# A decoder's first cross-attention: keys and values projected one stage earlier, during the state-space loop

## What is computed

```python
x = x + mamba(layernorm(x))          # per step: h = exp(delta*A)*h + delta*B*u ; y = sum over 8 states of C*h
# first cross-attention, 16 heads of 16
Q = layernorm(x) @ wq.T + bq
K = ctx @ wk.T + bk                  # ctx: 375 rows for each of 32 batch elements
V = ctx @ wv.T + bv
att = softmax(where(mask == 0, -1e-9, Q K^T / sqrt(16)))
x = x + (att @ V) @ wo.T + bo
x = x + switch_ffn(layernorm(x)); x = x + agent_attention(layernorm(x))
x = x + second_cross_attention(layernorm(x), ctx)   # other weights, same context
x = x + latent_moe(layernorm(x))
```

## Time and profile before

| | |
|---|---|
| median of 3 runs | 2842.92 us (2836.62 to 2844.70) |
| the profiled execution, its own time | 2844.52 us |
| its span, first to last instruction | 2842.7 us |
| TensorE busy | 2446.9 us (86%) |
| VectorE busy | 1947.9 us (69%) |
| ScalarE busy | 1565.1 us (55%) |
| bytes moved by DMA | 168.10 MB |

### The profile page before, as it was taken

One profiled execution on the slowest core, in us unless ns is written; L12 is line 12 of the kernel. 1 busy time (PEld: TensorE's weight loads), 2 busy tenths in 40 slices (PEclk: granted clock), 3 DMA queues, 4 the chain that ended last, 5 costly groups with the idle time before them and its releaser, 6 DMA issues. The chain is left out here.

```text
span 2842.7 us, 59554 instructions
## 1 busy us (share of the span) xinstructions
PE 2446.9 (86%) x20502; PEld 1684.8 (59%) x20503; DVE 1947.9 (69%) x4438; ACT 1565.1 (55%) x3006; POOL 461.1 (16%) x494
## 2 busy tenths in 40 slices
PE   7767877746899999999886899999999899969993
PEld 3333434323566676766674477777776555559993
DVE  2699999996577777777665477777777455662224
ACT  2666666651466666666373466666666233305553
POOL 0010000003100000000031211111110133224551
PEclk9878888867899999999886899999999799969997
DMA  4476666763000000000001000000000310002225
GB/s 110 104 160 158 157 159 156 157 156 76 17 22 16 22 16 22 16 22 11 1 16 40 8 23 22 22 22 22 22 22 6 114 32 16 17 22 65 70 70 177
DMA packets 84698, 168.10 MB, mean 59 GB/s; under 512 B 11040, under 2 KB 65730, under 8 KB 84354
## 3 DMA queue, kind: packets, MB, share of 16 engines
q0 software_dynamic: 15264, 75.25, 12.4%
q1 hardware_dynamic: 69330, 91.50, 10.9%
HBM read 92.17 MB, written 15.83 MB: 38 GB/s over the span
## 5 line engine op out<-in xcount | busy, mean ns | idle before, releaser
L1249 DVE CUSTOM_DVE_ANT_0 xa_h_scores<-xa_h_score_bank,xa_h_added 112x375 f32<-112x375 f32 x1024 | 518.1, 544 | 150.2 <-PE xa_h_score_bank L1184 127.5
L1343 ACT ACTIVATE xa_h_probs<-xa_h_scores,xa_h_negmax 112x375 f32<-112x375 f32 x1024 | 561.4, 600 | 0.9 <-DVE xa_h_negmax L1256 0.6
L1196 PEld LDWEIGHTS xa_h_turn_bank<-keep_ident,xa_h_probs 112*125 112x125 f32 x3072 | 396.1, 189 | 91.7 <-DVE xa_h_probs_t L1263 23.1
L1196 PE MATMUL xa_h_turn_bank<-keep_ident,xa_h_probs 112*125 112x112 f32 x3072 | 435.9, 278 | 9.3 <-DVE xa_h_probs_t L1263 9.1
L1263 DVE COPY xa_h_probs_t<-xa_h_turn_bank 125x448 f32<-125x448 f32 x512 | 319.1, 623 | 148.4 <-PE xa_h_turn_bank L1196 134.9
L1349 ACT ACTIVATE xa_h_probs_t<-xa_h_turn_bank 125x448 f32<-125x448 f32 x256 | 138.6, 541 | 301.1 <-PE xa_h_turn_bank L1196 301.0
L615 DVE TENSOR_TENSOR_SCAN mb_state<-mb_decay,mb_drive 128x1792 f32<-128x1792 f32 x64 | 248.5, 3883 | 0.8 <-ACT mb_decay L551 0.4
L1184 PE MATMUL xa_h_score_bank<-xa_h_keys,xa_h_queries 32*112 32x375 f32 x2048 | 231.6, 522 | 10.7 <-DVE xa_h_row_max L1249 10.0
L1209 PEld LDWEIGHTS xa_h_sums_bank<-xa_h_probs_t,xa_h_values 125*32 125x32 f32 x6144 | 141.1, 110 | 154.1 <-DVE xa_h_probs_t L1263 149.0
L423 PE MATMUL mb_front_bank<-mb_normed_t,mb_w_eff 128*128 128x448 f32 x512 | 207.9, 567 | 19.0 <-ACT mb_normed_t L508 18.4
L1209 PE MATMUL xa_h_sums_bank<-xa_h_probs_t,xa_h_values 125*32 125x112 f32 x6144 | 201.4, 264 | 14.5 <-issue 6.6
(11 more groups left out here) (354 smaller groups left out, 3864.9 us busy)
## 6 DMA issues: line engine op xcount, KB each, us to landing
mb_y<-mb_read_out POOLq DMA_DIRECT2D x64, 896.0 KB, 6.9
mb_rows<-mb_low_rows SPq DMA_DIRECT2D x64, 448.0 KB, 4.1
xa_context<-in_ctx_t SPq DMA_DIRECT2D x64, 375.0 KB, 3.1
lm_w<-in_m_w SPq DMA_DIRECT2D x16, 512.0 KB, 10.3
lm_e_wide<-lm_result_rows SPq DMA_DIRECT2D x8, 896.0 KB, 9.0
keep_x<-in_x SPq DMA_DIRECT2D x4, 896.0 KB, 15.6
lm_latent_rows<-lm_rows SPq DMA_DIRECT2D x8, 448.0 KB, 3.2
out_x<-keep_x SPq DMA_DIRECT2D x8, 448.0 KB, 6.1
```

The source lines that it names most:

```text
L1196: last = pe.transpose(turn_bank[(par + kc) % 2][0:KP, g * S:(g + 1) * S], probs[par][:, g, kc * KP:(kc + 1) * KP], keep.ident[0:S, 0:S])
L1249: dve.tensor_tensor_reduce(scores[par][:, g, :], score_bank[g][0:S, 0:SK], added[s][:, :], 1.0, -BIG, ALU.add, ALU.max, row_max[par][:, g: ...
L1343: act.activation(probs[par][:, g, :], scores[par][:, g, :], ACT.Exp, bias=negmax[s][:, G * c + g:G * c + g + 1]).then_inc(probs_ready, 1)
```

## The change

For each batch element t the state-space loop now also loads the context (375 KB), projects its keys and values on TensorE into four banks of their own (`keys_and_values`), reads them on ScalarE (`read_keys_and_values`) and stores them to DRAM: 375 KB of keys, and values as 125 x 816 floats, a column of ones for each head included. Four batch elements are handled in each group of the loop, at n = 1, 3, 4 and 6 on TensorE, at n = 2, 3, 5 and 7 on ScalarE. There is one buffer each for the context, the keys and the values. B and C rows now have two slots each and a transfer each; the B slot is free again after a drive, the C slot after a read-out.

The first attention's head loop no longer projects. SyncE loads keys and values of row t as soon as row t-2 is done with the buffers. `weigh` there writes 17 rows of the bank for each head (16 values and the sum) and not 32, and the bank is cleared once. The second cross-attention is as it was.

```diff
+        self.ctx_t, self.weights = ctx_t, weights
+        self.keys = nc.dram_tensor(name + "keys_rows", (B, 128, DC, SK), F32).ap()
+        self.values = nc.dram_tensor(name + "values_rows", (B, KP, KC, H, DK + 1), F32).ap()
 
...
-        low, rows = sb("low", [4 * LOW, T]), sb("rows", [128, ROW_SLOTS, 2, T])
+        low, b_rows, c_rows = sb("low", [4 * LOW, T]), sb("b_rows", [128, 2, T]), sb("c_rows", [128, 2, T])
+        context, keys_out, values_out = sb("context", [128, DC, SK]), sb("keys_out", [128, DC, SK]), sb("values_out", [KP, KC, H, DK + 1])
...
+        kv_bank = [psum(f"kv_bank{n}", [128, 512]) for n in range(KV_PARTS)]
...
-                reuse(sp, read_out_ready, N * g + n - ROW_SLOTS + 1)
+                reuse(sp, drive_ready, N * g + n - 1)
                 sp.sem_inc(load_started, 1)
-                sp.dma_start(rows[:, n % ROW_SLOTS, :, :],
-                             low_rows[bass.ds(g, 1), :, n, :].broadcast_to([128, 2, T])).then_inc(rows_in[n % ROW_SLOTS], 16)
+                sp.dma_start(b_rows[:, n % 2, :], low_rows[bass.ds(g, 1), 0, n, :].broadcast_to([128, T])).then_inc(b_in[n % 2], 16)
+                reuse(sp, read_out_ready, N * g + n - 1)
+                sp.sem_inc(load_started, 1)
+                sp.dma_start(c_rows[:, n % 2, :], low_rows[bass.ds(g, 1), 1, n, :].broadcast_to([128, T])).then_inc(c_in[n % 2], 16)
...
+            def load_context(t):
+
+                reuse(sp, kv_done, KV_PARTS * t)
+                sp.sem_inc(load_started, 1)
+                sp.dma_start(context[:, :, :], ahead.ctx_t[bass.ds(t, 1)].rearrange("o (c p) k -> p (o c) k", p=128)).then_inc(context_in, 16)
+
+            def store_keys_and_values(t):
+
+                sp.wait_ge(kv_read, KV_PARTS * t + 2)
+                sp.sem_inc(store_started, 1)
+                sp.dma_start(ahead.keys[bass.ds(t, 1)].rearrange("o p c k -> (o p) (c k)"), keys_out[:, :, :].rearrange("p c k -> p (c k)")
+                             ).then_inc(keys_stored, 16)
+                sp.wait_ge(kv_read, KV_PARTS * (t + 1))
+                sp.sem_inc(store_started, 1)
+                sp.dma_start(ahead.values[bass.ds(t, 1)].rearrange("o p c h v -> (o p) (c h v)"), values_out[:, :, :, :].rearrange("p c h v -> p (c h v)")
+                             ).then_inc(values_stored, 16)
...
             def group(g, k, at, final=False):
                 for n in range(N):
                     load_rows(g, n)
+                    if n == 0 and at != 0:
+                        load_context(G * g)
+                    if n == 1 and at != 0:
+                        store_keys_and_values(G * g - 1)
+                    if n == 3:
+                        load_context(G * g + 1)
+                    if n == 4:
+                        store_keys_and_values(G * g)
+                    if n == 5:
+                        load_context(G * g + 2)
+                        store_keys_and_values(G * g + 1)
+                    if n == 6:
+                        load_context(G * g + 3)
+                    if n == 7:
+                        store_keys_and_values(G * g + 2)
                 if not final:
                     store_low(g + 1)
...
 
+            load_context(0)
             store_low(0)
             all_groups(sp, group)
+            store_keys_and_values(B - 1)
+            sp.wait_ge(keys_stored, 16 * B)
+            sp.wait_ge(values_stored, 16 * B)
...
+            def keys_and_values(t):
+
+                wk, wv = ahead.weights.wk, ahead.weights.wv
+                pe.wait_ge(context_in, 16 * (t + 1))
+                for m in range(DC):
+                    reuse(pe, kv_read, KV_PARTS * (t - 1) + m + 1)
+                    for c in range(DC):
+                        last = pe.matmul(kv_bank[m][:, 0:SK], wk[:, c, m * 128:(m + 1) * 128], context[:, c, :], start=c == 0, stop=c == DC - 1)
+                    last.then_inc(kv_done, 1)
+                for part, chunks in ((2, (0, 1)), (3, (2,))):
+                    reuse(pe, kv_read, KV_PARTS * (t - 1) + part + 1)
+                    for j, kc in enumerate(chunks):
+                        for c in range(DC):
+                            last = pe.matmul(kv_bank[part][0:KP, j * D:(j + 1) * D], context[:, c, kc * KP:(kc + 1) * KP], wv[:, c, :],
+                                             start=c == 0, stop=c == DC - 1)
+                    last.then_inc(kv_done, 1)
...
@@ -469,12 +538,20 @@
                             turn_rows(g)
                     if 1 <= n < 5 and not final:
                         convolve(g, n - 1)
+                    if n == 1:
+                        keys_and_values(G * g)
+                    if n == 3:
+                        keys_and_values(G * g + 1)
+                    if n == 4:
+                        keys_and_values(G * g + 2)
                     if n == 5:
                         if not final:
                             low_rank(g)
                         project_out(g, 1 - k, 0) if not first else pass_over(OUT_A)
-                    if n == 6 and not final:
-                        deltas(g)
+                    if n == 6:
+                        if not final:
+                            deltas(g)
+                        keys_and_values(G * g + 3)
                     if n == 7:
...
+            pe.wait_ge(ahead.weights.loaded, ahead.weights.count)
             all_groups(pe, group)
...
+            def read_keys_and_values(t):
+
...
+                for m in range(DC):
+                    act.wait_ge(kv_done, KV_PARTS * t + m + 1)
+                    reuse(act, keys_stored, 16 * t)
+                    if bk is not None:
+                        act.activation(keys_out[:, m, :], kv_bank[m][:, 0:SK], ACT.Identity, bias=bk[:, m:m + 1]).then_inc(kv_read, 1)
...
+                reuse(act, values_stored, 16 * t)
+                act.activation(values_out[:, 0:2, :, 0:DK], kv_bank[2][0:KP, 0:2 * D].rearrange("p (c h v) -> p c h v", c=2, h=H),
+                               ACT.Copy).then_inc(kv_read, 1)
+                act.wait_ge(kv_done, KV_PARTS * (t + 1))
+                act.activation(values_out[:, 2, :, 0:DK], kv_bank[3][0:KP, 0:D].rearrange("p (h v) -> p h v", h=H),
+                               ACT.Copy).then_inc(kv_read, 1)
...
@@ -562,23 +658,30 @@
                         read_low(g)
                     if n + 2 < N:
                         decays(g, n + 2)
-                    if final:
-                        continue
                     if n == 2:
-                        read_inner(g, (0, 1))
-                    if n == 3 and at != GROUPS - 2:
-                        normalise_rows(g + 2)
-                    if n == 4:
+                        if not final:
+                            read_inner(g, (0, 1))
+                        read_keys_and_values(G * g)
+                    if n == 3:
+                        if not final and at != GROUPS - 2:
+                            normalise_rows(g + 2)
+                        read_keys_and_values(G * g + 1)
+                    if n == 4 and not final:
                         read_inner(g, (2, 3))
-                    if n == 6:
+                    if n == 5:
+                        read_keys_and_values(G * g + 2)
+                    if n == 6 and not final:
                         softplus(g)
                     if n == 7:
+                        read_keys_and_values(G * g + 3)
+                    if n == 7 and not final:
                         decays(g + 1, 0)
                         decays(g + 1, 1)
...
                 dve.wait_ge(state_ready, N * g + n + 1)
+                dve.wait_ge(c_in[n % 2], loads_of_rows(g, n))
                 dve.tensor_tensor(read_out[:, n % 2, :, :], state[:, n % 2, :, :],
-                                  rows[:, n % ROW_SLOTS, 1, :].unsqueeze(1).broadcast_to([128, IC, T]), ALU.mult).then_inc(read_out_ready, 1)
+                                  c_rows[:, n % 2, :].unsqueeze(1).broadcast_to([128, IC, T]), ALU.mult).then_inc(read_out_ready, 1)
...
+            def load_context(t, s):
+                sp.wait_ge(proj_done, place(t - 3, "values2") + 1)
+                sp.dma_start(context[s][:, :, :], ctx_t[bass.ds(t, 1)].rearrange("o (c p) k -> p (o c) k", p=128)).then_inc(context_in[s], 16)
+
+            def load_keys_and_values(t, s):
+                sp.wait_ge(scores_done, NQ * (t - 1))
+                sp.dma_start(keys[s][:, :, :], stored.keys[bass.ds(t, 1)].rearrange("o p c k -> (o p) c k")).then_inc(keys_in[s], 16)
+                sp.wait_ge(weighed, NQ * (t - 1))
+                sp.dma_start(values[s][:, :, :, :], stored.values[bass.ds(t, 1)].rearrange("o p c h v -> (o p) c h v")).then_inc(values_in[s], 16)
+
+            load = load_context if projected else load_keys_and_values
             for t in (2, 3):
-                sp.wait_ge(proj_done, place(t - 3, "values2") + 1)
```

(15 more changed lines are left out.)

92 lines of the change are left out of this document (61 added, 31 removed).

## The result

The change makes the kernel slower by half a per cent. The median of 8 runs is 2858.68 us (2846.35 to 2865.84), against 2842.03 us for the kernel before (8 runs, 2836.62 to 2844.70): a ratio of 1.0053, with a 95% interval of 1.0032 to 1.0075. I had forecast 2833. The measured time is 25.7 us above that and lies within the range of 2800 to 2880, but on the side to which I gave 0.31.

A forecast was written before the change was run, and what follows sets the result against it. The prediction took VectorE to bound the state-space loop and TensorE the head loop. From 2844.5 us, attention gave -66.3 and the state-space loop +55.3, making 2833.5, less a little for the median: 2833 us, range 2800 to 2880.

The forecast's parts named there:

- Row transfers: State-space loop: late B rows stall VectorE 1 to 5 us at steps 5 and 6, hidden; costed at nothing.
- Additions to y: State-space loop: added loads and stores lengthen the additions' cycle from 7.8 to at most 9.9 us; costed at nothing.
- the limit of 9.9: State-space loop: cycle of an addition to y, in us, up to which the last read-out need not wait.
- the first rival: State-space loop: value stores on few engines lengthen additions to y, read-out of step 7 waits; 2878 us, chance 0.27.
- The chain: State-space loop: projections delay convolutions, low-rank product and softplus on TensorE and ScalarE; group 77.7 us, +55.3 us in sum.
- Head loop: First attention without projections: row 18.21 us instead of 19.94, saving 53.6 us, and 12.7 at the start.
- third rival: Head loop: TensorE's clock falls to 1.2 GHz in stretches, +3.9 us a row, 2953 us; chance 0.03.
- The better fit: State-space loop: TensorE's clock rises to full as gaps fill, a group grows by only 4 us; 2806 us, chance 0.18.

The follow-up runs named there:

- e4: Changed kernel with all its matmuls and reads, but only the first context loaded and only the last keys and values stored: 2838.4 us, ratio 0.9967 to 0.9990.
- e3: Changed kernel, but values stored from and loaded to all 128 partitions in place of 125: 2839.7 us, ratio 0.9980 to 1.0007.
- e9: Changed kernel with B row issued first and projections in half blocks off the way to the low-rank product, values on 125 partitions: 2855.7 us.

## Why the prediction was wrong

The step that failed is "Row transfers", with its sentence "VectorE may stall 1 to 5 us at steps 5 and 6, but it has 5.4 us to lose before `add_to_x`. Costed at nothing". The mechanism was right and the size was not, and a second cost, at the end of group 7, was missing. Against the sum the profiled span is 31.7 us too long: 21.0 in groups 0 to 6, where B rows were late, 12 to 14 in group 7 and 10.6 in the steps of the head loop, less 14.2 in stages that the change leaves alone.

- **Row transfers.** I took 4.1 us for a transfer of a row and "more" for the others beside it, without a number. Rows that were waited for took up to 14.8 us. In group 3 the two waits were 3.4 and 9.3 us, in group 5 they were 4.0 and 8.1, against a cover of 5.4. The cover was no fixed amount either. It is what VectorE would have waited for anyway, and e4 shows it: 9.1 and 7.0 us at `add_to_x` in groups 1 and 2, whose first convolutions ran at the lower clock, but 3.6 to 5.5 in groups 3 to 6, with 1.5 to 1.9 more at delta in each. So 10.3 and 7.8 us of late B rows cost nothing in groups 1 and 2; groups 0 to 2 last as long as in e4 (78.2, 81.9, 79.3 against 77.8, 82.2, 79.2). The other four took 325.7 us against e4's 304.4. There VectorE waited 41.0 us for B rows and 3.0 for softplus, where e4 has 16.7 for the output projection and 6.4 for softplus: 20.9 us more, nearly the whole difference. My price without cover was 7 x 3 = 21 us, and the excess is 21.5. That these agree is luck: the waits were 68.6 us over seven groups, not 21, and the cover took up the rest.
- **Additions to y.** Costed at nothing and right up to group 6: they landed in 8.3 us, 9.2 with the issue, below the limit of 9.9. Not right for the end of group 7, which I had at 0 to +2. There the last addition was awaited for 14.1 us (6.6 before), B rows for 4.9 and the additions at the read-out for 1.1, and the group grew by 13.9 us in all; e4, without the transfers, has +2.3. I had looked at the additions only where a read-out waits for them, not at the last `finish`, which waits for all eight.
- **The rule I set aside.** For values on 125 partitions I wrote that the sum would move towards the first rival and then left it where it was. e3 shows that this one number was worth 19 us in the medians. The rival put the cost at the read-out; it fell on the B rows, and only e9, with a shorter chain, has it at the read-out.
- **The chain.** Right in what it is made of, and in its sum partly by luck: e4 gives 543.5 us for 544.0, but by group it has 82.2 and 79.2 in groups 1 and 2 and 75.5 to 77.4 in groups 3 to 6, where I had 77.7 in each. The lower clock and the late start in the first ones and the full clock in the others happened to cancel. The low-rank product started at 50.2 to 52.3 in groups 2 to 6 of the change and at 55.3 in group 1 (50 to 51 forecast), and group 0's delta at 173.8 (173.4).
- **Head loop.** The row is 18.36 (18.21 forecast), the plain steps 3.87 (3.88), the start -12.8 (-12.7). What was missing is 7.9 us in five steps at the lower clock. That is most of the 10.6 by which the gain fell short. My third rival had this mechanism but priced it for every row. I took row 31 as proof against it, a row too short to show a fall that comes once in six.

The better fit failed as a rival: the clock rose as it says (0.94 in group 3), but the 50.6 of the chain already held most of what that brings. Where the convolutions ran at the full clock throughout, as in e4, a group took 75.6, not 74.
